# Two-layer decoder, local attention stage: weights transposed in two halves of the tokens, maxima as steps of their own, another order of work

## The reference, cut to what matters

```python
h = layernorm(x)                                   # (2, 1024, 256)
q, k, v = split(h @ Wqkv.T)                        # 16 heads of 16
q, k = rope(q), rope(k)                            # pairs (2i, 2i+1), base 10000
s = q @ k.T / sqrt(16), masked to 0 <= i - j <= 128
x = x + (softmax(s) @ v) @ Wproj.T + bproj
```

## Time and profile before

| | |
|---|---|
| median of 3 runs | 2547.52 us (2543.78 to 2550.26) |
| profiled execution, its own time | 2545.91 us |
| its span | 2543.8 us |
| PE busy | 2262.9 us (89% of the span) |
| DVE busy | 1633.5 us (64%) |
| ACT busy | 1135.2 us (45%) |
| POOL busy | 736.0 us (29%) |

### The profile page before, as it was taken

One profiled execution on the slowest core, in us unless ns is written; L12 is line 12 of the kernel. 1 busy time (PEld: TensorE's weight loads), 2 busy tenths in 40 slices (PEclk: granted clock), 3 DMA queues, 4 the chain that ended last, 5 costly groups with the idle time before them and its releaser, 6 DMA issues. The chain is left out here.

```text
span 2543.8 us, 62618 instructions
## 1 busy us (share of the span) xinstructions
PE 2262.9 (89%) x26115; PEld 1870.4 (74%) x26115; DVE 1633.5 (64%) x3577; ACT 1135.2 (45%) x3176; POOL 736.0 (29%) x866
## 2 busy tenths in 40 slices
PE   5798989998898999955998589989997899999998
PEld 4677877777785888844887366666775788888887
DVE  6766666667644667656784455655665777777776
ACT  4444443443324555522554356656674233333332
POOL 2333333424323433331565433420111011110110
PEclk9899999999999999966999799999998899999999
DMA  5000000100103000020442300000000000000001
GB/s 159 4 17 30 32 31 11 35 27 25 51 3 111 10 18 18 14 80 26 119 119 34 105 2 2 2 2 2 2 2 14 19 26 26 26 20 26 26 7 34
DMA packets 87961, 83.36 MB, mean 33 GB/s; under 512 B 27264, under 2 KB 83456, under 8 KB 86272
## 3 DMA queue, kind: packets, MB, share of 16 engines
q1 hardware_dynamic: 81536, 70.98, 8.9%
q0 software_dynamic: 6144, 8.39, 1.9%
HBM read 68.71 MB, written 10.65 MB: 31 GB/s over the span
## 5 line engine op out<-in xcount | busy, mean ns | idle before, releaser
L2653 PE MATMUL bank<-f_XH,f_wp 128*128 128x512 f32 x1088 | 364.6, 396 | 5.9 <-DVE f_XL L2763 5.9
L797 DVE SCALAR_TENSOR_TENSOR a_acc<-a_praw,a_convw,a_acc 128x256 f32<-128x256 f32 x345 | 206.7, 600 | 97.6 <-ACT a_acc L957 89.4
L2653 PEld LDWEIGHTS bank<-f_XH,f_wp 128*128 128x128 f32 x1088 | 208.4, 192 | 48.6 <-issue 5.0
L2653 PEld LDWEIGHTS bank<-f_wp,f_Hp 128*128 128x128 f32 x1632 | 214.3, 191 | 27.5 <-DVE X L2790 16.0
L2653 PE MATMUL bank<-f_wp,f_Hp 128*128 128x256 f32 x1632 | 218.5, 283 | 16.2 <-DVE X L2790 15.4
L2653 PE MATMUL bank<-f_XL,f_wp 128*128 128x512 f32 x544 | 215.9, 397 | 0.0
L2837 POOL TENSOR_TENSOR f_wp<-wa,f_wp 128x768 fp32r<-128x768 f32 x34 | 62.9, 1849 | 521.6 <-ACT f_wp L2803 521.6
L2788 DVE SCALAR_TENSOR_TENSOR X<-bank,f_w,X 128x256 f32<-128x256 f32 x512 | 211.4, 475 | 0.0
L2826 ACT ACTIVATE f_Hp<-f_H 128x512 fp32r<-128x512 f32 x136 | 85.9, 632 | 223.8 <-DVE f_H L2775 223.8
L2824 ACT ACTIVATE f_G<-bank 128x512 f32<-128x512 f32 x136 | 81.3, 598 | 165.2 <-PE bank L2653 165.2
L2777 DVE TENSOR_TENSOR f_Hp<-f_H,f_Hp 128x512 fp32r<-128x512 f32 x136 | 94.1, 692 | 94.9 <-ACT f_Hp L2826 94.9
(11 more groups left out here) (389 smaller groups left out, 5530.2 us busy)
## 6 DMA issues: line engine op xcount, KB each, us to landing
wa<-in_c_w SPq DMA_DIRECT2D x64, 256.0 KB, 3.4
wa<-in_f_gu SPq DMA_DIRECT2D x34, 256.0 KB, 2.8
wb<-grown SPq DMA_DIRECT2D x4, 1536.0 KB, 6.9
a_KQg<-grown SPq DMA_DIRECT2D x4, 1536.0 KB, 6.4
wa<-in_f_d SPq DMA_DIRECT2D x34, 128.0 KB, 2.8
a_E<-decays SPq DMA_DIRECT2D x16, 256.0 KB, 4.0
X<-in_x SPq DMA_DIRECT2D x4, 512.0 KB, 5.2
wa<-in_a_wqkv SPq DMA_DIRECT2D x1, 2048.0 KB, 8.8
```

Source lines behind the costliest of these rows:

```text
L797: i = v.e.scalar_tensor_tensor(A_, praw[:, c, :, j:j + BT_], convw[:, c, j:j + 1], A_, ALU.mult, ALU.add)
L2653: i = t.e.matmul(out_, lhsT[x], rhs[y], start=n == 0 and k == 0, stop=n == 2 and k == nk - 1, skip_group_check=True)
```

## The change

In stage D:

- **Turn.** The transposes of the weights are made for `r` in pairs (`h` = 0, 1) and each block of 128 tokens by 128 keys is split in two halves of 64 tokens: a transpose of rows 0 to 63 and one of rows 64 to 127, in row tiles of their own of the array, each half into a bank of its own. ACT copies the first half of every pair, DVE the second; `PT` is laid out anew for it.
- **Maxima.** `max` is an entry of its own: DVE does maxima 0 and 1, then the copy of the second transposes, then the step's other work, with maxima 2 and 3 among it; exps 2 and 3 follow them.
- **Order.** `flip` follows the scores directly; `project` stands right behind the second transposes, ahead of `across` and the last exps. `norm` stands at the beginning of a step and its `ln` at the end.
- **Head.** Only normalizations 0 and 1 stand ahead of the loop, in place of four; the others ride in steps 2 to 7. The rotation of project 0 is done by DVE with the same four operations; the others stay with POOL. `bo` gets a semaphore of its own, and the projection no longer waits for it. The memsets and the cast of the window mask stand first in the stage on their engines.

```diff
-            PT = [t_(f"PT{i}", [P, 2, 2 * P]) for i in range(NPB)]
+            PT = [t_(f"PT{i}", [P, 2, 2, 2, P]) for i in range(NPB // 2)]
-            lns = [[("stat", "D", i)] * (i < 4) + [("norm", "D", i - 1), ("ln", "D", i - 1)] * (i > 0) for i in range(5)]
-            order = lns[0] + lns[1] + [("project", 0), ("project", 1)] + lns[2] + [("keys", 0, 0), ("keys", 0, 1)] + lns[3] + lns[4]
+            order = [("stat", "D", 0), ("stat", "D", 1), ("norm", "D", 0), ("ln", "D", 0), ("norm", "D", 1), ("project", 0)]
+            order += [("ln", "D", 1), ("keys", 0, 0), ("keys", 0, 1), ("project", 1)]
             for g in range(G + 3):
                 m, n = g // 2, g // 2 - 2
-                turn = [("turn", g - 1, r) for r in range(4)] if 0 <= g - 1 < G else []
-                scores, exps = ([(what, g, r) for r in range(4)] if g < G else [] for what in ("score", "exp"))
+                turn = [("turn", g - 1, h) for h in range(2)] if 0 <= g - 1 < G else []
+                scores, maxima, exps = ([(what, g, r) for r in range(4)] if g < G else [] for what in ("score", "max", "exp"))
                 across = [("across", g - 2)] * (0 <= g - 2 < G)
-                order += [("stat", "D", g + 3)] * (1 <= g < 5)
-                order += turn[0:2] + [("mix", g - 2)] * (0 <= g - 2 < G)
-                order += scores + exps[0:1]
+                order += [("stat", "D", g + 1)] * (1 <= g < 7) + [("norm", "D", g)] * (2 <= g < 8)
+                order += turn[0:1] + [("mix", g - 2)] * (0 <= g - 2 < G) + scores
+                order += [("flip", n)] * (g % 2 == 0 and 0 <= n < NT) + maxima[0:2] + exps[0:2] + turn[1:2]
                 if g % 2 == 0:
-                    order += [("flip", n)] * (0 <= n < NT) + turn[2:3] + exps[1:2] + turn[3:4] + exps[2:4] + across
-                    order += [("keys", m + 1, 0), ("keys", m + 1, 1)] * (m + 1 < NT) + [("out", n)] * (0 <= n < NT)
+                    order += across + [("keys", m + 1, 0), ("keys", m + 1, 1)] * (m + 1 < NT) + maxima[2:3] + exps[2:3]
+                    order += [("out", n)] * (0 <= n < NT) + maxima[3:4] + exps[3:4]
...
                 else:
-                    order += turn[2:3] + exps[1:2] + turn[3:4] + exps[2:4] + [("project", m + 2)] * (m + 2 < NT)
-                    order += across + [("values", m)] * (m < NT)
-                if 1 <= g < 5:
-                    order += [("norm", "D", g + 3), ("ln", "D", g + 3)]
+                    order += [("project", m + 2)] * (m + 2 < NT) + across + maxima[2:3] + exps[2:3] + [("values", m)] * (m < NT)
+                    order += maxima[3:4] + exps[3:4]
+                order += [("ln", "D", g)] * (2 <= g < 8)
...
+                    if what == "turn":
+                        _, g, h = s
+                        for half in range(2):
+                            free(t, *s, half)
+                        for r in range(2):
+                            emptied(t, "score", g, 2 * h + r)
+                            for j in range(2):
+                                for kt in tiles(g // 2):
+                                    for half, rows_ in enumerate(halves):
+                                        b = at[s + (half,)]
+                                        i = t.e.transpose(by_group(b.ap)[:, r, j, kt, :],
+                                                          Pm[of(g, 2 * h + r)][rows_, j, kt * P:(kt + 1) * P],
+                                                          ident[rows_, rows_], tile_position=(rows_.start, 0))
+                                        if (r, j, kt) == (1, 1, 1):
+                                            i.then_inc(b.filled, 1)
...
-                        t.wait_ge(w_in, 48)
+                        t.wait_ge(w_in, 32)
...
+            def rotate(e, n):
+                ...the four operations that stood in gpsimd(), now on engine e...
...
+                    elif s == ("project", 0):
+                        rotate(v, 0)
...
             def gpsimd(g):
                 fence(g, "D")
+                for i in range(2):
+                    g.e.memset(qk[i][:, :, :, :], 0.0)
+                g.e.memset(V[:, :, :, AD + 1:], 0.0)
+                g.e.memset(V[:, :, :, AD:AD + 1], 1.0).then_inc(cleared, 1)
```

More of the change, by code:

```diff
@@ L2005, in stage_d @@
                     i = s[-1]
-                    max_ready.mark(*s[1:])
+                elif what == "turn":
+                    for half in range(2):
+                        at[s + (half,)] = banks[4 + turns % 4]
+                        at[s + (half,)].turn(*k, half)
+                        turns += 1
+                    continue
                 else:
@@ L2031, in tensor @@
                     what, b = s[0], at.get(s)
-                    if what in ("exp", "bias", "shut", "stat", "norm"):
+                    if what in ("max", "exp", "bias", "shut", "stat", "norm"):
                         continue
@@ L2073, in tensor @@
                         continue
-                    elif what == "turn":
-                        _, g, r = s
-                        emptied(t, "score", g, r)
-                        for j in range(2):
-                            for kt in tiles(g // 2):
-                                i = t.e.transpose(pair(b.ap)[:, j, kt * P:(kt + 1) * P],
-                                                  Pm[of(g, r)][:, j, kt * P:(kt + 1) * P], ident)
                     elif what == "mix":
@@ L2084, in tensor @@
                         emptied(t, "values", n)
-                        for r in range(4):
-                            emptied(t, "turn", g, r)
+                        for h in range(2):
+                            for half in range(2):
+                                emptied(t, "turn", g, h, half)
                         for j in range(2):
@@ L2111, in tensor @@
                     i.then_inc(b.filled, 1)
+            def rotate(e, n):
+                r3, o3 = (x[:, :].rearrange("p (h d) -> p h d", d=AD) for x in (raw, rot))
+                r4, o4 = (x[:, :].rearrange("p (h d i) -> p h d i", h=2 * AH, i=2) for x in (raw, rot))
+                turn = sin[:, n % TB, :].rearrange("p (d i) -> p d i", i=2)
+                both = [P, 2 * AH, AD // 2]
+                emptied(e, "project", n)
+                e.e.tensor_tensor(o4[:, :, :, 0], r4[:, :, :, 1], turn[:, :, 0].unsqueeze(1).broadcast_to(both), ALU.mult)
+                e.step(e.e.tensor_tensor(o4[:, :, :, 1], r4[:, :, :, 0], turn[:, :, 1].unsqueeze(1).broadcast_to(both),
+                                         ALU.mult)); e.settle()
+                e.step(e.e.tensor_tensor(r3, r3, cos[:, n % TB, :].unsqueeze(1).broadcast_to([P, 2 * AH, AD]),
+                                         ALU.mult)); e.settle()
+                e.wait_ge(cleared, 1)
+                if n > 1:
+                    filled(e, "keys", n - 2, 1)
+                e.e.tensor_tensor(qk[n % 2][:, :, :, 0:AD].rearrange("p a h d -> p (a h) d"), r3, o3,
+                                  ALU.add).then_inc(rotated.sem, 1)
             def vector(v):
@@ L2199, in scalar @@
                         if g > 1:
-                            filled(c, "turn", g - 2, r)
+                            for half in range(2):
+                                filled(c, "turn", g - 2, r // 2, half)
                         c.wait_ge(max_ready.sem, max_ready.at[g, r])
@@ L2205, in scalar @@
                         i.then_inc(b.emptied, 1)
-                    elif what == "turn" and s[2] < 2:
-                        _, g, r = s
-                        lo = P if len(tiles(g // 2)) == 1 else 0
+                    elif what == "turn":
+                        _, g, h = s
+                        b, kts = at[s + (0,)], slice(tiles(g // 2)[0], 2)
                         if g > 1:
                             filled(c, "mix", g - 2)
-                        filled(c, *s)
-                        c.e.activation(PT[of(g, r)][:, :, lo:], pair(b.ap)[:, :, lo:], ACT.Copy).then_inc(b.emptied, 1)
+                        filled(c, *s, 0)
+                        c.e.activation(PT[of(g, 2 * h) // 2][:, :, :, kts, halves[0]], by_group(b.ap)[:, :, :, kts, :],
+                                       ACT.Copy).then_inc(b.emptied, 1)
                     elif what == "mix":
```

57 lines of the change are left out of this document (23 added, 34 removed).

## The result

| | before | after |
|---|---|---|
| median of 5 runs each | 2547.52 us (2543.78 to 2550.26) | 2535.91 us (2532.24 to 2543.15) |
| ratio, 95% interval | | 0.9959 [0.9945, 0.9973] |
| profiled execution, its own time | 2545.91 us | 2537.03 us |
| its span | 2543.8 us | 2534.8 us |
| stage D, from `X` back to stage E's first weight matmuls | 306.18 us | 294.60 us |

The kernel became faster by 11.6 us (the interval allows 7 to 14), about half of the 22.8 forecast. The median before is of five runs; the table ahead of the prediction, which gives the same figures, calls them three. Stage D shrank by 11.6 in the profiled pair as well; the span fell by only 9.0, because in that one execution the stages behind D, whose code is untouched, took 5.3 us more, and those ahead of it 2.7 less. What is known of that stands at the end.

What follows compares the result with a forecast made beforehand. The head was taken as a chain of waits, the loop as bound by PE with short stops. Terms -8.7 + 2.2 - 0.5 - 6.1 + 0.6 - 9.8 - 0.5 sum to -22.8 us, giving 2525, range 2514 to 2540.

Steps and rivals of the forecast that it cites:

- The head: Start of stage D up to the first window matmul: first window about 1424.3, 8.7 us earlier (7.3 to 10.3).
- Step 0: First loop step: `keys 1` waits for project 1's rotation on POOL, so 7.8 us in place of 5.6, +2.2.
- Step 1: Second loop step: gains 0.5 us because project 2 no longer has DVE's late copies before it.
- Steps 2 to 7: Early loop: steps 2 to 4 -6.1 us without `ln` waiting for `norm`; steps 5 to 7, now carrying `ln`, +0.6.
- The transposes: PE's half transposes in the loop: 0.062 us a pair, a group of eight pairs 0.54 in place of 0.97.
- Rival 1: Loop transposes: a half pair costs a full load, 0.112 us; total -12.5, 2535 us; chance 0.21, shared with an ineffective split.
- The odd step: Loop steps with `values`, starting 5.15 us in: 7.3 + T = 7.84 us, T being a group of transposes.
- The even step: Loop steps with `keys`, second half at 5.15 us: 7.9 + T = 8.44 us, or 8.5 by the exp 3 chain.
- Rival 2: Loop: late exps bound it, maxima 2 and 3 waiting behind `keys` and `out`; even steps 9.0, 2532 us; chance 0.10.
- A pair of steps: Loop, one even and one odd step together: 16.4 us against 17.25, -0.85 a pair.
- the two boundary steps: Loop at the batch boundary: two steps counted as half, within 11.5 pairs and -9.8 us for steps 8 to 31.
- The tail: End of stage D, after 1696.8 us: -0.5 us.

Runs made afterwards that it cites:

- e8: Kernel after with `across` before `project`, `values` before maximum 2, ACT's copy of the second turns between exps 0 and 1, rotation 1 on DVE; 2502.92 us.
- e2: Kernel after with `values` ahead of maximum 2 and exp 2 in odd steps, so ACT copies `V` before exp 2; 2524.33 us, ratio 0.9910.
- e3: Kernel after with `across` ahead of `project` in odd steps; 2526.74 us, ratio 0.9922.
- e1: Kernel after with whole 128x128 transposes in place of the halves, the new order kept; 2536.17 us, ratio 0.9963.
- e7: Kernel after with the rotation of project 0 back on POOL; 2536.66 us in one run.
- e5: e2 with whole 128x128 transposes in place of the halves; 2529.62 us, ratio 0.9921.
- e6: e2 with ACT's copy of the second turns moved between exps 0 and 1; 2509.22 us, ratio 0.9846.
- e4: Kernel before with only the new head, and `norm` at the start and `ln` at the end of a step; 2539.72 us, ratio 0.9973.
- e9: e8 with whole 128x128 transposes in place of the halves; 2514.30 us, ratio 0.9874.

## Why the prediction came out too low

**The head: right, 1.3 us too generous in this execution.** The projection started 7.95 us after the stage began (forecast 8.3), `keys` at 14.8 (forecast 15.1): memsets, cast, statistics and rotation 0 on DVE (2.3 us for its four operations, 2.5 forecast) hold. The cast was held by the memsets as suspected, and came out of it at 1.19 us in place of 0.34. The missing pieces are the last two: `keys` took 1.73 to the start of `project 1` where 1.1 were given, and `project 1` 3.42 to the first window where 1.7 to 2.6 were. The whole stretch shows a granted clock of 0.50, the lower of the two levels, 1.2 GHz, where before it was 0.62; I had given the two terms prices of a mixed clock. The other eight kernels with this head and rotation 0 on DVE show 0.59 to 0.61 there and take 18.84 to 19.10 us, within 0.4 of the forecast 18.7.

**Step 0: the reason right, the number in part luck.** 7.86 against 7.8, and e8, which moves rotation 1 off POOL, takes 5.0. But the sum had no term for the clock, which was 0.72 here: e2 and e3, with the same instructions in this step, took 7.17 and 6.95 at 0.92 and 0.96. **Step 1: wrong in sign,** +2.8 in place of -0.5. Its stretch shows a granted clock of 0.65; e1 and e2 took 7.55 and 7.38 for it at 0.84 and 0.85, so about 2 us go with the clock. The forecast knew neither that nor what keeps even those 0.7 to 0.9 over before.

**Steps 2 to 7: right,** -7.0 against -5.5. No `ln` waits for `norm` any more, which was 1.24 us at the end of step 3.

**The transposes: right.** Sixteen half transposes take 0.71 us with 0.23 for the last, that is (0.71 - 0.23)/15 = 0.032 each and 0.064 a pair (forecast 0.062); with the following switch 0.64 to the next matmul (forecast 0.54 + 0.10). Their loads last 139 ns as those of the whole ones did (143), and L739's, for the same 64x128 weights, 198. The Trainium skill, "TensorE: Matmul & The Clock Gate", LDWEIGHTS, makes a load's time a matter of its columns alone: the pair 139 and 143 agrees with that, and the pair 139 and 198, equal in columns and rows, doesn't. The rule's consequence, no gain from halves, did not come: at 139 ns a load and 0.032 us from one to the next, loads of the two row halves overlap. How I came to 0.062, L739's pair less the difference of one load, is not shown by any run; the number fits, the working stays a guess. Rival 1 named the time that was measured, 2535, but not its reason.

**The odd step: the step that failed.** The prediction wrote "Odd: values at 5.15, then 1.05 + 0.1 + T + 1.0 = 7.3 + T = 7.84". Measured: `values` at 5.27, then 1.06 + 0.64 + **0.69** + 1.01 = 8.67. Each term is right to 0.12 but one that isn't in the sum: between the transposes and `mix` the wait for `V`. I had followed the banks and the exps to the *next step's* windows, and `keys` to the scores, but `mix` I let start when PE was ready, because in the earlier trace rows it never waited. Before, all exps of the step stood well ahead of the copy of `V`; the change put `values` behind `maxima 2` and `exp 2` in the list. The copy's own queue was the thing to trace, and then that of the instruction ahead of it. e2 removes the wait, and the odd step becomes 7.78 to 7.99, around the forecast 7.84. The wait accounts for 7.8 of the 11.2 us that were missing (e2's steps 8 to 30 against e7's); counted with these alone the change would have given 19.4. That e2's whole stage is 25.8 us shorter than before, past the 22.8 forecast, is luck in part: 6.4 of its 14.2 lie elsewhere, most of them where its clock was the higher one.

**The clock: a term put at nothing in the loop and in steps 0 and 1.** Against other executions of the same work, or nearly the same in step 1, the low clock cost the kernel after 0.7 to 0.9 us in step 0 (e2, e3), about 2 in step 1 (e1, e2) and 1.6 in steps 29 and 30 (e7). It is a second, smaller failed term beside the wait, and the order of work can't be blamed for the last of these: e7 has the same order.

**The even step: better than forecast,** 8.17 against 8.44 to 8.5, with the wait at `keys` ended by ACT's copy as forecast. Rival 2 (even steps at 9.0) did not occur. A pair of steps gained 0.41 to 0.52 in place of 0.85.

**What had no term:** the batch boundary, +1.1 (step 19 takes 9.26 in place of 8.31, with 0.42 of waiting for the last exp and 0.76 for `V`; in e2 it is 8.43), and step 29, 8.38 in place of 7.57, in which the clock falls (0.76 over 1670 to 1677 us): the 32 matmuls of `mix` (L2111) take 1.88 us in place of 1.08. PE stopped 1.04 and 0.80 us just before the fall. Those stops alone don't bring it: e7 has both, at a clock of 1.00 throughout, and takes 7.58 and 6.71 for steps 29 and 30; e3 has both and the fall. The kernel after, then e7:

```profile
1672.80 1.88 PE L2111 MATMUL bank<-d_PT,d_V 128*32 128x128 f32 x32 [0.80 <-ACT d_V L2227]
```

```profile
1678.12 1.08 PE L2111 MATMUL bank<-d_PT,d_V 128*32 128x128 f32 x32 [0.80 <-ACT d_V L2225]
```

Why some executions fall there and others don't stays open. I priced the two boundary steps at half a pair's gain. The tail was put at -0.5 without any working; it gave +0.4.

The account of steps 8 to 30: steps 8 to 15 gave -1.9 and steps 20 to 28 -2.6, eight and a half pairs at a little over half their forecast; steps 16 to 18 gave +0.1, step 19 +0.95, step 29 +0.8 and step 30 nothing. Together -2.6. At e7's clock step 29 would have given nothing and step 30 -0.9.

## What to carry to other kernels

When an entry of a common order is moved, follow it on every engine, and ask of each *result* that comes later who copies it out, what stands ahead of the copy in that engine's list, and what that in turn waits for. A wait absent from the old trace isn't a wait that can't come: it means only that the old order left slack there. And price a saving on the bounding engine only together with the stops behind it: here the same half transposes were worth 4.7 us of steps 2 to 30 with the wait for `V`, 4.7 without it and 8.0 once the wait at `keys` was cut too, and three moved entries with one more rotation on DVE were worth nearly three times the whole change. Take what an edit is worth from steps that ran at the same granted clock in both kernels: whole stages differed by several microseconds at places that the edit did not touch.

## What the hardware showed that I had not expected

- **The granted clock decides a few microseconds outside the change.** The first 29.4 us of stage E, whose code didn't change, ran at a mean granted clock of 0.84 after and 1.00 before; all of stage E took 224.8 and 219.5 us. The stretches after, then before:

```profile
1697.60:1727.00 29.40, 28.06 (x155) 17.68 (x154) 11.41 (x22) 12.75 (x31) 5.08 (x10) 0.84 0.01 2
1697.57:1922.37 224.80, 212.56 (x2465) 155.61 (x2464) 131.66 (x328) 145.18 (x401) 26.23 (x59) 0.96 0.01 2
```

```profile
1711.85:1741.25 29.40, 27.59 (x196) 17.67 (x198) 14.40 (x30) 15.49 (x40) 5.07 (x10) 1.00 0.01 2
1711.85:1931.35 219.50, 207.28 (x2466) 152.30 (x2464) 131.59 (x328) 144.91 (x401) 26.16 (x59) 0.99 0.01 2
```

  The stages behind D took 831.8 to 833.5 us in before, e2, e5, e6, e7 and e8, and 836.0 to 837.3 in after, e1, e3, e4 and e9, whatever the edit. Over the runs of one kernel the time goes with the mean granted clock: e4 took 2550.34 us at 0.943 and 2534.40 at 0.951, the kernel after 2543.15 at 0.943 and 2532.24 at 0.950. So one profiled pair can be off by more than the change moved; the stage's own length is what to compare. What starts the low stretch at the beginning of E in some executions stays open.
- **POOL's memset holds DVE's cast.** The cast of the window mask, 128x384 to bf16, took 0.34 us alone before (at 1414.17) and 1.19 beside the memset that started 0.02 us after it; the `norm` beside memsets took 2.86 in place of 0.73. The Trainium skill, "SBUF — State Buffer", Who interferes with whom, says that DVE's copies, casts and tensor-scalars in their faster modes and a GpSimd operation take one pair of ports in turn; these numbers agree with it, except that the cast, 0.02 us ahead of the memset in the records, was still the one held. Transfers don't explain it: the DMA share was 1.14 beside the quick cast (1414.1 to 1414.6 us, before) and 0.91 beside the slow one. Putting memset and cast both first in a stage therefore costs about 0.85 us.
- **Half transposes run at nearly twice the rate of whole ones.** 0.032 us from start to start for 64x64 of float32 in alternating row halves, 0.064 a pair, where a whole transpose took 0.11 and a record of L739's non-transposing matmuls, of the same shape, 0.056. With the longer gaps beside a half group (0.06 to 0.09 us), a group of eight is 0.23 cheaper and not 0.33.
